# Raw expert weights issued from the sync queue, and four small moves, in a two-layer mixture-of-experts kernel

## The chip, the cores and the metric

The kernel runs on one core of a Trainium2 chip. The metric is the device time of one launch in microseconds. The engines of the core are TensorE (PE in the profile), VectorE (DVE), ScalarE (ACT), GpSimd (POOL) and the sync engine (SP); each runs its own list of instructions in order and waits on semaphores. SP and ACT can each put DMA transfers on a hardware queue of their own, GpSimd on a software queue.

## What is computed

An input of 16 images, 256 channels and 16x16 pixels goes through two layers. Each has a token mixer (a gated group convolution in the first, a 1x1 convolution in the second) and then a feed-forward network with eight experts, of which every token takes two. What matters here is the second feed-forward network, and the 1x1 convolution ahead of it:

```python
x = x + _L1_conv_ref(_ln_c(x), L1_conv_weight, L1_conv_bias)
t = _to_tokens(x)
t = t + _L1_ffn_ref(_ln_t(t), L1_ffn_gate_w, L1_ffn_gate_b, L1_ffn_w1, L1_ffn_b1, L1_ffn_w2, L1_ffn_b2)
# inside _L1_ffn_ref: 4096 tokens, d=256, F=1024, E=8, K=2
router = jax.nn.softmax(xf @ gate_w + gate_b, axis=-1)
k_scores, k_idx = jax.lax.top_k(router, K)
for i in range(e):
    h = jax.nn.silu(xf @ w1[i] + b1[i])
    y = h @ w2[i] + b2[i]
    out = out + y * comb[:, i:i + 1]
```

The first feed-forward network has the same routing, F=512 and a gated form, silu(x w1) * (x w3), then w2.

## The kernel before

Both networks are computed sparsely, and `f` is 0 in the first and 1 in the second. `route(f)` chooses experts and makes lists of the tokens of each expert, padded to tiles of 256 tokens; here that gives 35 tiles in each network, and a table `bounds` with the first tile of each expert. The loops over experts are unrolled, the loops over an expert's tiles are hardware loops whose ends are read from `bounds` at run time.

A tile `n` goes through these hands. GpSimd gathers its 256 rows from HBM (`fetch`, two indirect DMAs, for the two halves r of a tile; the first three tiles in `first_fetch`, the rest in a loop). SP turns them with two DMA transposes (`turn_rows`) into one of four buffers of `x_cols` (`RING` is 4): it turns tile n+4 once TensorE has finished the first products of tile n (`z_ready`). TensorE does the first products (L809) and the second ones (L824 in the first network, L836 in the second). ScalarE applies Silu (L1141, L1146) and scales results (L1122, L1161), VectorE splits the hidden values into a high and a low half in fp16 (L1692, L1695) and takes the result out of PSUM (L1707). GpSimd adds the result rows to `rows_y` in HBM (`put`, two indirect DMAs with addition, L562). In the second network there is only one result buffer `y_rows`: VectorE's L1707 of a tile waits (`y_free`) until both puts of the tile before have landed.

TensorE multiplies fp16 pairs, so every expert's weights are needed as high and low halves. The second network's weights are 2 MB per expert; three raw buffers `raw_v` hold them as fp32, and expert e uses buffer e % 3. `load_raw(eng, e)` issues four DMAs of 512 KB (lines 319 and 322). Expert 0 is split between the layers, the halves of expert e+1 are made one small part per tile while expert e runs (`loop_highs` on ScalarE, `loop_lows` on VectorE, counted by `part_lo`), and what is left over is done by VectorE in `rest_of` ahead of the next expert's tiles.

Where the raw weights are issued, before: ScalarE issues expert 0 behind the tiles of expert 0 of the first network (last lines of `experts`), experts 1, 2 and 3 in `route(1)` between `deviation(3, 0)` and `result_columns(5)`, and experts 4 to 7 in `next_raw` at the head of experts 1 to 4.

Other places in question: GpSimd loads the second gate's bias `gate_b` (first network) and the result biases `b2_all` (1 MB, second network) between `first_fetch(1)` and `first_fetch(2)`, and VectorE waits for them at the head of `experts`. TensorE's first products of the first network wait for a count (`hid_ready`) that VectorE sets behind that wait. SP loads the row `bias_rows` ahead of `load_tokens(0)`, which brings the tokens back between the layers; GpSimd adds that row to the tokens (L619).

## Time and profile before

| | us |
|---|---|
| median of 3 timed runs | 1178.34 (1178.17 to 1178.98) |
| profiled execution, its own time | 1181.54 |
| its span | 1179.8 |
| TensorE busy | 883.0 (75%) |
| VectorE busy | 752.3 (64%) |
| ScalarE busy | 583.7 (49%) |
| GpSimd busy | 504.1 (43%) |
| first network's tiles begin | 313.5 |
| second network's tiles begin | 758.5 |

Times of rows are in us from the start of the span. In a row of the timeline stand the start, the length, the engine, the line, the operation, what it writes and reads, how many instructions were merged into the row, and in brackets how long the engine had been idle before it and who ended that. In a row of the chain (the chain of work that ended last, followed back from the end) stand the start, the length and what it was. "q" behind an engine's name is its sequencer, which issues DMAs and takes its own time for that.

### The profile page before, as it was taken

Reading aid. Unit: us, or ns where it says so; the run is one execution under the profiler, and the core shown is the slowest. Engines: PE = TensorE matmul, PEld = TensorE weight load, DVE = VectorE, ACT = ScalarE, POOL = GpSimd, SP = SyncE. Lnnn points to the kernel's source line nnn. Section 1 sums busy time; section 2 is a strip of 40 time slices with the busy share of each in tenths; the row PEclk is TensorE's granted clock in tenths of the full one; section 3 lists DMA queues with packets and bytes.
Section 4 is the critical chain, followed back from the end, with each engine's and each line's share of the span. In section 5 each row is a group of like instructions: output and inputs, shape, how many; then the busy total and the mean of one; then the engine's idle time right before and its main releaser. Section 6 shows DMA issues by size and latency. Waiting matters only on the chain.

```text
span 1179.8 us, 25135 instructions
## 1 busy us (share of the span) xinstructions
PE 883.0 (75%) x7033; PEld 743.8 (63%) x7033; DVE 752.3 (64%) x1826; ACT 583.7 (49%) x1251; POOL 504.1 (43%) x412
## 2 busy tenths in 40 slices
PE   5321186865597999999956344499999999999975
PEld 4101165861386888888845231287888888888863
DVE  5999788989342444444446589467676677667540
ACT  4447285854162454444442247255455456555433
POOL 1288000000344676666663120245565555556540
PEclk8755598975598999999987775599999999999996
DMA  8249265982246555555654646336546464344438
GB/s 259 72 143 320 71 234 177 285 268 46 64 80 120 103 98 99 99 102 94 103 86 146 213 143 153 86 72 139 134 76 143 92 122 77 71 72 76 76 61 286
DMA packets 196628, 152.23 MB, mean 129 GB/s; under 512 B 97056, under 2 KB 181480, under 8 KB 196456
## 3 DMA queue, kind: packets, MB, share of 16 engines
q1 hardware_dynamic: 143736, 91.70, 27.6%
q0 software_dynamic: 27472, 38.97, 19.8%
q10 hardware_dynamic: 25376, 21.04, 6.3%
q8 instruction: 20, 0.33, 0.1%
q14 instruction: 24, 0.20, 0.1%
HBM read 92.35 MB, written 39.91 MB: 112 GB/s over the span
## 4 chain that ended last, share of the span: by engine, by line
PE 38%; DMA 22%; DVE 18%; issue 10%; SPq 4%; ACT 4%; ACTq 2%; POOL 1%; DVEq 1%; POOLq 0%
PE bank L836 15%; PE bank L809 13%; DMA columns<-region 8%; DMA region<-rows_x,region 7%; SPq L416 3%; PE bank L891 2%; DVE columns L1287 2%; DVE region L1266 2%; PE bank L713 2%; DVE region L1264 1%; DMA rows_y<-region 1%; DVE wreg L1632 1%; PE bank L791 1%; DVE wreg L260 1%; DMA out_dram<-columns 1%
## 5 line engine op out<-in xcount | busy, mean ns | idle before, releaser
L809 PE MATMUL bank<-columns,wreg 128*128 x3360 | 384.9, 275 | 37.0 <-DMA columns<-region 22.7
L809 PEld LDWEIGHTS bank<-columns,wreg 128*128 128x128 f16 x3360 | 331.3, 99 | 80.1 <-issue 38.5
L562 POOL DMA_INDIRECT rows_y<-region x140 | 240.5, 1718 | 166.7 <-ACT region L1161 98.5
L509 POOL DMA_INDIRECT region<-rows_x,region x148 | 156.6, 1058 | 261.1 <-DVE region L1564 144.8
L836 PE MATMUL bank<-wreg,region 128*128 128x256 f16 x1680 | 189.3, 273 | 12.4 <-DVE region L1695 12.4
L836 PEld LDWEIGHTS bank<-wreg,region 128*128 128x128 f16 x1680 | 163.2, 98 | 34.7 <-DVE region L1695 15.7
L1146 ACT ACTIVATE region<-bank,b_t,wreg 128x256 f32<-128x256 f32 x280 | 136.5, 562 | 35.8 <-PE bank L809 35.8
L1700 DVE TENSOR_TENSOR region<-region 128x256 f16<-128x256 f32 x140 | 50.1, 421 | 106.2 <-ACT region L1153 106.2
L1695 DVE SCALAR_TENSOR_TENSOR region<-region,wreg 128x512 f16<-128x512 f32 x140 | 105.3, 752 | 5.0
L1161 ACT ACTIVATE region<-region 128x256 f32<-128x256 f32 x70 | 31.8, 500 | 154.1 <-DVE region L1707 154.1
L824 PE MATMUL bank<-wreg,region 128*128 (+1 forms) x864 | 100.2, 273 | 1.9 <-ACT region L1153 1.9
L1692 DVE TENSOR_SCALAR region<-region,wreg 128x512 f16<-128x512 f32 x140 | 70.5, 504 | 46.3 <-ACT region L1146 46.3
L1141 ACT ACTIVATE region<-bank,fac 128x256 f32<-128x256 f32 x140 | 62.3, 474 | 67.4 <-PE bank L809 67.3
L824 PEld LDWEIGHTS bank<-wreg,region 128*128 128x128 f16 x864 | 84.4, 98 | 12.0 <-ACT region L1153 2.2
L1122 ACT ACTIVATE region<-bank,region 128x256 f32 x72 | 30.2, 471 | 100.3 <-DMA rows_y<-region 81.0
L1689 DVE SCALAR_TENSOR_TENSOR region<-bank,fac,region 128x256 f32<-128x256 f32 x140 | 58.9, 478 | 10.0 <-ACT region L1141 10.0
L557 POOL COPY region<-routed 128x4 uint32 x70 | 60.8, 869 | 7.3 <-DMA region<-rows_x,region 7.3
L769 PE MATMUL bank<-columns 128*128 128x160 f16 x128 | 38.6, 314 | 32.4 <-DVE columns L1538 28.3
L947 ACT ACTIVATE wreg<-wreg 128x1024 f32<-128x1024 f32 x56 | 58.5, 1053 | 2.6 <-DMA wreg<-in_L_ffn_w_dram 2.2
L1707 DVE SCALAR_TENSOR_TENSOR region<-bank,wreg,region 128x512 f32<-128x512 f32 x35 | 26.3, 751 | 49.4 <-PE bank L836 42.0
L891 PE MATMUL bank<-conv_wt,columns 128*128 128x272 f32 x128 | 37.2, 442 | 24.9 <-DVE wreg L1394 24.9
L1586 DVE SCALAR_TENSOR_TENSOR wreg<-wreg (+1 forms) x68 | 47.7, 747 | 6.3 <-ACT wreg L1091 4.2
(284 smaller groups left out, 1148.9 us busy)
## 6 DMA issues: line engine op xcount, KB each, us to landing
wreg<-in_L_ffn_w_dram SPq DMA_DIRECT2D x80, 512.0 KB, 5.8
wreg<-in_L_ffn_w_dram ACTq DMA_DIRECT2D x32, 512.0 KB, 7.4
rows_x<-region SPq DMA_DIRECT2D x16, 512.0 KB, 6.9
rows_y<-tok SPq DMA_DIRECT2D x16, 512.0 KB, 6.8
tok<-rows_y SPq DMA_DIRECT2D x16, 512.0 KB, 6.0
wreg<-in_x_dram SPq DMA_DIRECT2D x4, 1024.0 KB, 9.8
out_dram<-columns ACTq DMA_DIRECT2D x16, 256.0 KB, 2.4
region<-rows_x,region POOLq DMA_INDIRECT x148, 2.9
```

The lines of the kernel that those rows point to most:

```text
L509: nc.gpsimd.indirect_dma_start(x_bits[:, b, r, 0:C + 2], None, rows_x[f], bass.IndirectOffsetOnAxis(ap=row_list, axis=0)).then_inc(xr_load ...
L557: nc.gpsimd.tensor_copy(now[:, b], moves[:, bass.ds(2 * t, 2), :]).then_inc(lists_copied[f], 1)
L562: nc.gpsimd.indirect_dma_start(rows_y[f], bass.IndirectOffsetOnAxis(ap=now[:, b, g_, 1:2], axis=0), (y_pair[:, b], y_rows)[f][:, g_, :], N ...
L809: last = pe.matmul(to, block, x_cols[:, bass.ds(b, 1), :, xs_, k, :].rearrange("p j r n -> p (j r) n"), start=(k == 0 and ws_ + xs_ == 0), ...
L824: last = pe.matmul(yb[:, r * C:(r + 1) * C], lhs[:, r * P:(r + 1) * P], w2_of(c, ws_), start=(c == 0 and r == 0 and hs + ws_ == 0), stop=( ...
L836: last = pe.matmul(yb[:, r * C:(r + 1) * C], lhs[:, c, r * P:(r + 1) * P], v_s[:, e % 2, c // 2, 1, ws_, (c % 2) * C:(c % 2 + 1) * C], sta ...
L891: last = pe.matmul(zb[2 * j + h][:, 0:C + 2 * E], xt[:, j, k, h * P:(h + 1) * P], conv1_wt[:, k], start=(k == 0), stop=(k == KC - 1))
L1141: act.activation(gate_act[:, h, (c % 2) * TILE:(c % 2 + 1) * TILE], zb[c][:, 0:TILE], ACT.Silu, scale=fac[f][:, 0, e:e + 1]).then_inc(silu ...
L1146: last = act.activation(gate_act[:, h, c * TILE:(c + 1) * TILE], zb[h][:, c * TILE:(c + 1) * TILE], ACT.Silu, bias=b1_t[:, e, 2 * h + c:2 ...
L1689: dve.scalar_tensor_tensor(half(hid[:, h], c), zb[c][:, TILE:2 * TILE], fac[f][:, 1, e:e + 1], half(gate_act[:, h], c), ALU.mult, ALU.mult ...
L1692: dve.tensor_scalar(to_hi, gate_act[:, h], fac[f][:, 1, e:e + 1], None, ALU.mult).then_inc(hi_ready[f], 1)
L1695: dve.scalar_tensor_tensor(to_lo, gate_act[:, h], fac[f][:, 1, e:e + 1], to_hi, ALU.mult, ALU.subtract).then_inc(lo_ready[f], 1)
```

## The change

It has five parts. The raw weights are issued by SP: expert 0 ahead of the turning loop of the first network, experts 1 and 2 behind `load_tokens(0)`, expert 3 ahead of the turning loop of the second network, experts 4 to 7 behind the turns of experts 0 to 3, once the parts of the last tile are made. VectorE's wait for `gate_b` stands behind the first network's tiles, and its wait for `b2_all` at the head of `experts` is gone (the wait in front of L1707 counts the same semaphore). `first_fetch(2)` stands ahead of the loads of `gate_b` and `b2_all`. ScalarE does one Silu of one column ahead of the tiles. The row `bias_rows` is loaded behind the fourth of the eight token loads.

```diff
             def load_tokens(f):
                 for i in range(HB):
+                    if f == 0 and i == 4:
+                        sp.dma_start(bias_rows[:], ...).then_inc(bias_loaded, 16)
...
+            def turn_behind(f, first, end):
+                with sp.Fori(first, end) as n:
+                    sp.wait_ge(z_ready[f], 4 * n + 4)
+                    turn_rows(f, n + RING)
             def turn_tiles(f):
...
-                with sp.Fori(0, total + 2 - RING) as n:
-                    sp.wait_ge(z_ready[f], 4 * n + 4)
-                    turn_rows(f, n + RING)
+                if f == 0:
+                    sp.wait_ge(w_lo, 6 * E)
+                    load_raw(sp, 0)
+                    turn_behind(0, 0, total + 2 - RING)
+                else:
+                    sp.wait_ge(v_lo, 4)
+                    load_raw(sp, 3)
+                    edges = [sp.value_load(bounds[0:1, e:e + 1], min_val=0, max_val=TILES) for e in range(5)]
+                    for e in range(4):
+                        turn_behind(1, edges[e], edges[e + 1])
+                        with sp.Fori(edges[e + 1], edges[e + 1] + 1) as n:
+                            sp.wait_ge(part_lo, n + 1)
+                        load_raw(sp, e + 4)
+                    turn_behind(1, edges[4], total + 2 - RING)
...
-            sp.dma_start(bias_rows[:], ...).then_inc(bias_loaded, 16)
             load_tokens(0)
+            for e in (1, 2):
+                load_raw(sp, e)
...
                 first_fetch(1)
+                first_fetch(2)
                 if f == 0:
                     (loads of gate_b)
                 else:
                     pool.dma_start(b2_all, b2.partition_broadcast(P)).then_inc(y_free, 16)
-                first_fetch(2)
...
                     deviation(3, 0)
-                    for e in (1, 2, 3):
-                        load_raw(act, e)
                     result_columns(5)
...
             def experts(f, edges):        # ScalarE
                 act.wait_ge(fac_ready[f], 1)
+                act.activation(spare_column, fac[f][:, 0, 0:1], ACT.Silu)
...
-                    if f == 1 and 0 < e and e + 3 < E:
-                        next_raw(e + 3, edges[e])
...
-                    if f == 0 and e == 0:
-                        load_raw(act, 0)
...
             def experts(f, edges):        # VectorE
-                for loaded in (y_put, [y_free])[f]:
-                    dve.wait_ge(loaded, 16)
...
             experts(0, edges)
+            for b in range(2):
+                dve.wait_ge(y_put[b], 16)
             first_lows()
```

ScalarE in `route(1)`, before, between the layers. L995 is `result_columns`, L921 a square root of `deviation`, L1005 and L1009 are `result_rows`, L319 and L322 `load_raw`:

```order
L995 ACTIVATE columns<-bank 128x512 x6
L921 ACTIVATE rstd<-var 128x16
L319 DMA wreg<-in_L_ffn_w_dram 128x2x512 x2
L322 DMA wreg<-in_L_ffn_w_dram 128x4x256 x2
L319 DMA wreg<-in_L_ffn_w_dram 128x2x512 x2
L322 DMA wreg<-in_L_ffn_w_dram 128x4x256 x2
L319 DMA wreg<-in_L_ffn_w_dram 128x2x512 x2
L322 DMA wreg<-in_L_ffn_w_dram 128x4x256 x2
L995 ACTIVATE columns<-bank 128x512 x2
```

And with the change (the same lines are L1016, L942, L1026 and L1030):

```order
L1016 ACTIVATE columns<-bank 128x512 x6
L942 ACTIVATE rstd<-var 128x16
L1016 ACTIVATE columns<-bank 128x512 x2
L1026 ACTIVATE wreg<-tok,mean,rstd 128x256 x4
L1030 ACTIVATE region<-wreg 128x2x256 x2
```

Twelve DMA instructions no longer stand between the square root and the columns.

SP in the second network, before, from the turns of tile 3 into the turning loop:

```order
L416 DMA_TRANSPOSE columns<-region 128x4x128 [waits xr_loaded0_1,xc_ready0_1]
L416 DMA_TRANSPOSE columns<-region 128x4x128 [waits xr_loaded1_1,xc_ready1_1]
L426 UNCONDITIONAL_BRANCH
L426 ISA
L265 ISA [waits z_ready1]
```

With the change, from the turns of the last tile of expert 0's loop to the head of expert 1's (L419 is the turn, L445 the wait for the parts, L320 and L323 are `load_raw`):

```order
L419 DMA_TRANSPOSE columns<-region 128x4x128
L419 ISA [waits xr_loaded1_1,xc_ready1_1]
L419 DMA_TRANSPOSE columns<-region 128x4x128
L423 REGISTER_ALU
L423 COMPARE_AND_BRANCH
L445 UNCONDITIONAL_BRANCH
L445 ISA
L445 ISA [waits part_lo]
L445 COMPARE_AND_BRANCH
L320 DMA wreg<-in_L_ffn_w_dram 128x2x512 x2
L323 DMA wreg<-in_L_ffn_w_dram 128x4x256 x2
L423 UNCONDITIONAL_BRANCH
```

The four loads stand behind the turns of the tile that is four ahead of the expert's last one, and ahead of every later turn.

ScalarE at the head of the second network's tiles, before and then with the change:

```order
L1135 UNCONDITIONAL_BRANCH
L1135 ISA
L1146 ACT_TABLE_LOAD
L1146 ACTIVATE region<-bank,b_t,wreg 128x256 x2
```

```order
L1142 ACT_TABLE_LOAD
L1142 ACTIVATE wreg<-wreg 128x1
L1147 UNCONDITIONAL_BRANCH
L1147 ISA
L1158 ACTIVATE region<-bank,b_t,wreg 128x256 x2
```

The load of the table stood inside the loop over expert 0's tiles and now stands ahead of it; the first network's shows the same.

## Rows read from the trace of the kernel before

**Rows 1.** Timeline of TensorE, first network, tile 0 and the one stall.

```profile
313.54 8.26 PE L809 MATMUL bank<-columns,wreg 128*128 x48 [13.74 <-DVEq L1668]
...
364.47 6.73 PE L809 MATMUL bank<-columns,wreg 128*128 x48 [8.61 <-DMA columns<-region]
...
373.65 5.40 PE L809 MATMUL bank<-columns,wreg 128*128 x48
```

**Rows 2.** Chain of work, first network: gate bias, and a turn at the stall.

```profile
309.75 3.54 DMA gate_b<-in_L_ffn_gate_b_dram
352.33 11.75 DMA columns<-region
```

**Rows 3.** Line 416 (the turns) in the window 307.7 to 309: issue, then landing.

```profile
L416 SPq DMA_TRANSPOSE columns<-region x2: 1250/1280/1309, 306.6 to 308.0; - x2
DMA to landing us min/median/max: 3.3/3.3/3.3
```

**Rows 4.** Timeline of ScalarE: first raw DMA of expert 0.

```profile
349.38 0.69 ACTq L319 DMA_DIRECT2D wreg<-in_L_ffn_w_dram  x1
```

**Rows 5.** Timeline of GpSimd: the first put of the first network.

```profile
334.75 1.67 POOL L562 DMA_INDIRECT rows_y<-region  x1 [11.70 <-ACT region L1122]
```

**Rows 6.** Timelines of ScalarE, then VectorE, between the layers.

```profile
668.02 1.09 ACT L995 ACTIVATE columns<-bank 128x512 f32<-128x512 f32 x2 [11.69 <-issue]
...
675.24 0.25 DVE L1215 RECIPROCAL st_lg<-wreg 128x16 f32<-128x16 f32 x1 [9.93 <-ACT wreg L921]
```

**Rows 7.** Chain of work: last put of network one, bias row; turn at network two.

```profile
612.59 3.96 DMA rows_y<-region
617.74 0.37 SPq L436
...
753.28 4.93 DMA columns<-region
```

**Rows 8.** Timelines, second network, expert 0: TensorE, then ScalarE's table load.

```profile
777.11 5.45 PE L836 MATMUL bank<-wreg,region 128*128 128x256 f16 x48 [0.46 <-DVE region L1695]
788.25 5.41 PE L836 MATMUL bank<-wreg,region 128*128 128x256 f16 x48 [0.45 <-DVE region L1695]
...
773.42 1.28 ACT L1146 ACT_TABLE_LOAD   x1
```

**Rows 9.** Timeline of TensorE at the change to expert 5, which has no load.

```profile
1000.64 5.41 PE L836 MATMUL bank<-wreg,region 128*128 128x256 f16 x48 [1.76 <-DVE region L1695]
```

**Rows 10.** Timeline of VectorE: first split behind the change to experts 1 to 4.

```profile
810.95 0.48 DVE L1692 TENSOR_SCALAR region<-region,wreg 128x512 f16<-128x512 f32 x1 [0.72 <-ACT region L1146]
844.24 0.49 DVE L1692 TENSOR_SCALAR region<-region,wreg 128x512 f16<-128x512 f32 x1 [1.50 <-ACT region L1146]
899.68 0.48 DVE L1692 TENSOR_SCALAR region<-region,wreg 128x512 f16<-128x512 f32 x1 [1.18 <-ACT region L1146]
943.71 0.49 DVE L1692 TENSOR_SCALAR region<-region,wreg 128x512 f16<-128x512 f32 x1 [1.28 <-ACT region L1146]
```

**Rows 11.** Timeline of TensorE: second stall behind a change of expert.

```profile
857.28 5.41 PE L836 MATMUL bank<-wreg,region 128*128 128x256 f16 x48 [1.06 <-DVE region L1695]
911.98 5.41 PE L836 MATMUL bank<-wreg,region 128*128 128x256 f16 x48 [0.31 <-DVE region L1695]
956.79 5.41 PE L836 MATMUL bank<-wreg,region 128*128 128x256 f16 x48 [1.09 <-DVE region L1695]
```

**Rows 12.** Chain of work: a put beside a raw load that began at 895.8.

```profile
899.26 8.57 DMA rows_y<-region
```

**Rows 13.** Timelines of TensorE and GpSimd, an undisturbed tile of the second network.

```profile
867.77 5.40 PE L836 MATMUL bank<-wreg,region 128*128 128x256 f16 x48
878.16 1.86 POOL L562 DMA_INDIRECT rows_y<-region  x1 [0.30 <-issue]
883.12 0.98 POOL L509 DMA_INDIRECT region<-rows_x,region  x1 [0.30 <-issue]
```

**Rows 14.** The page's DMA issues: all gathers, median us to landing.

```profile
region<-rows_x,region POOLq DMA_INDIRECT x148, 2.9
```

More of the change, by code:

```diff
@@ L118, in bass_metaformer @@
         marks = region[:, 7861:7863]
+        spare_column = wreg[:, 32464:32465]
         raw_at = (24576, 16384, 20480)
@@ L389, in load_tokens @@
                 for i in range(HB):
+                    if f == 0 and i == 4:
+                        sp.dma_start(bias_rows[:], bias.rearrange("c a -> (c a)").partition_broadcast(P)).then_inc(bias_loaded, 16)
                     if i >= 4:
@@ L435, in _ @@
                     sp.wait_ge(waited, each * m + more)
-            sp.dma_start(bias_rows[:], bias.rearrange("c a -> (c a)").partition_broadcast(P)).then_inc(bias_loaded, 16)
             load_tokens(0)
+            for e in (1, 2):
+                load_raw(sp, e)
             for waited, each, more in ((xc_ready[0][0], 16, 32), (xc_ready[1][0], 16, 32)):
@@ L1107, in loop_highs @@
                 part_highs(e, (n - first) % 4).then_inc(part_hi, 1)
-            def next_raw(e, first):
-                with act.Fori(first, first + 1) as n:
-                    act.wait_ge(part_lo, n + 1)
-                load_raw(act, e)
             def result_of_last(n):
```

## The prediction

> **What bounds the kernel now.** I read the page's 40 slices first, then the chain of work, then each engine's timeline where the chain leaves TensorE. Four things hold TensorE or VectorE up, and raw loads or their neighbours stand beside all four.
>
> In the first network TensorE begins at 313.54, behind a wait of VectorE [rows 1], and the chain shows what that was: the gate bias, issued at 309.75, landing 3.54 later [rows 2]. Tile 5 then begins after 8.61 us idle, and its first products last 6.73 where those of the next tile last 5.40, at a lower granted clock [rows 1]. The chain has a turn issued at 352.33 that took 11.75 to land [rows 2], where a turn of the first tile took 3.3 [rows 3]; ScalarE had issued 2 MB of raw weights from 349.38 on [rows 4].
>
> Between the layers ScalarE's next arithmetic behind its twelve raw DMAs comes at 668.02, after 11.69 idle that is put down to issue (so from 656.3 on), and VectorE waited 9.93 for the square root behind it, until 675.24 [rows 6]. From there to the second network the chain is mostly VectorE's routing, which the change leaves alone.
>
> In the second network TensorE is the bound where nothing disturbs it: 5.24 us for each half of a tile, 10.48 a tile (each row shows 5.40, as ends are modelled) [rows 13]. It loses a little in expert 0, at every change of expert, and once more a tile later.
>
> **The change part by part.** All terms are us against the profiled execution (1181.54 for a span of 1179.8); the median of the runs is 1178.34, and I take the same difference off the median.
>
> Gate bias: VectorE no longer waits. What is late next is the turn of tile 0: the second transpose is issued at 308.0 and lands 3.3 later [rows 3], 311.3, so TensorE starts near 311.6: gain 1.9. GpSimd now waits for the bias itself ahead of its first list, some 1 to 2 us behind that tile's gather, but its first put comes only at 334.75 after 11.70 idle [rows 5]; that idle time hides it.
>
> Raw expert 0: SP issues it behind the turns of tile 3. The gather of tile 3 is GpSimd's last ahead of that idle time, which begins at 323.05 (334.75 less 11.70) [rows 5]; it lands 2.9 after its issue [rows 14], so the load starts near 327 less the 1.9 won. It lasts some 12 us (a put beside such a load landed 12.1 behind its start, below), so it is nearly through when the gather behind the first pair of puts starts, and a result is double buffered here. The stall goes: 8.61 and the slow 1.33 (6.73 less 5.40) [rows 1], 9.9 in all. If gather 4 is caught by its end I lose up to 3.
>
> Bias row: one issue of 0.37 less ahead of the token loads [rows 7], 0.4. GpSimd needs it only after VectorE's first statistics, so its later landing is hidden.
>
> Raw experts 1 to 3 leave ScalarE. Its work from 668.02 to VectorE's start at 675.24 is 7.2 us; started at 656.4 it ends at 663.6, before VectorE asks at 665.3 (675.24 less 9.93) [rows 6]. What is late next is VectorE itself, then a usual wait of some 0.3: gain 9.6. Experts 1 and 2 now follow the token loads on SP, where nothing is waited for until VectorE's first fp16 rows are stored, and those come behind the square root.
>
> Result biases: the turn that starts the second network took 4.93 beside 1 MB of them [rows 7]; 3.3 is the nearest undisturbed one [rows 3]: gain 1.6. They are next needed by the first L1707, more than a tile's 10.48 after TensorE's start.
>
> Silu table: ScalarE loads it in every pass of expert 0's loop, 1.28 each. In the second network tiles there are 11.14 apart (777.11 to 788.25) [rows 8], against 10.48: 0.66 for three tiles, 2.0. In the first network TensorE has no gap there: nothing.
>
> ScalarE's loads at the changes to experts 1 to 4: VectorE's first split waited 0.72, 1.50, 1.18 and 1.28 for ScalarE [rows 10], together 4.7 (4.68). VectorE's `rest_of` is late next and no load helps that: the change to expert 5 has no load and still costs 1.76 [rows 9].
>
> Sum of gains: 1.9 + 9.9 + 0.4 + 9.6 + 1.6 + 2.0 + 4.7 = 30.1.
>
> What it adds: five raw loads (experts 3 to 7) run in the second network where four did, and at another moment. Count from E, the end of a tile's second products (873.0 in the undisturbed tile). Its second put is issued at E+5.15, the gather four tiles on at E+10.1 [rows 13], landing 2.9 later [rows 14], near E+13; only then does SP get past the turns of that tile and issue the raw load. E of the next tile is 10.5 (10.9 at a change of expert) later, so the raw load starts 3.7 after it and the next pair of puts is issued 0.6 before and 1.4 behind its start. VectorE's L1707 needs those puts at 10.6. Undisturbed a put lands in 3.96 [rows 7], at 9.1, in time. Beside a raw load begun at 895.8 it took 8.57 from 899.26 [rows 12], so it landed 12.1 behind the load's start. By the length it lands at 5.15 + 8.57 = 13.7, 3.1 late; by the raw load's end at 3.7 + 12.1 = 15.8, 5.2 late. Against this, the raw load now follows the turns instead of sharing with them, so it may be through sooner. About 0.8 of lateness is slack (a put 2 us late cost TensorE 1.06 and 1.09 [rows 11]). So a stall lies between 0 and 4.4 for each load; I take 2.3, what the row's own length gives: 5 x 2.3 = 11.5. The three old stalls of 1.06, 0.31 and 1.09 [rows 11] go, 2.5. Net loss 9.0. The turns behind a raw load are one to two tiles late at most, and the ring holds them three tiles ahead.
>
> 30.1 less 9.0 is 21.1, and 1178.3 less 21.1 is 1157.2.
>
> A rule speaks to the sharing. The row shows a turn on SP's queue held for 11.75 behind a raw load on ScalarE's [rows 2, 4]. The Trainium skill, "DMA: Bandwidth & Descriptors", section "Queues, rings and completion order", says that each DMA engine goes round the queues it has work for, packet by packet, while one queue is consumed in order. By that a short turn on a queue of its own should have landed long before the end of the load, which the row does not bear out. For a put it would mean that it lands ahead of the raw load's end once the turns share the load's queue; that is the first rival.
>
> **The rivals.** *Puts keep their pace.* With load and turns on one queue, the put's queue has one competitor instead of two; it lands at 10.6 to 12 and a stall costs what the old ones did, 2.5/3 = 0.8. Then 5 x 0.8 - 2.5 = 1.6 is lost and 28.5 gained: 1149.8. For it: only three of four old loads stalled a second time. Against: 8.57 at 899.26 [rows 12]. The skill's rule of round robin points here.
>
> *Every put waits for the load's end.* If that is 13 behind its start, the put lands at 16.7, 6.1 late, a stall is 5.3: 26.5 - 2.5 = 24.0 lost, 6.1 gained: 1172.2.
>
> *Slower than before.* The same mechanism with a longer load: what is issued beside it lands with its end, and SP's queue serves it more slowly than ScalarE's. Break-even is a stall of (30.1 + 2.5)/5 = 6.5, a put landing 14.2 behind the load's start. At 16 the stall is 8.3: 41.5 - 2.5 - 30.1 = 8.9 lost, 1187.2. Against: beside the old load nothing in the rows took longer than 11.75 [rows 2] or landed later than 12.1 to 14.7 behind its start (352.33 + 11.75 less 349.38).
>
> *The change does not free ScalarE between the layers.* If the square root waits for something else there, 9.6 is missing: 1166.8. Against: the 11.69 idle is put down to issue, with no releaser, and the DMAs fill it [rows 6].
>
> **How the numbers follow.** Forecast 1157.2 (1152 to 1162 with its own bounds) 0.45; puts keep their pace, 1149.8, 0.25; puts wait for the end, 1172.2, 0.17; ScalarE not freed 0.05; slower 0.04; the rest for things in between. The range takes in the first rival with the 2.5 of stalls gone altogether (30.1 + 2.5 is 1145.7, half way to it is 1147) and stops at 1170 just short of the second. Faster by over 0.2% (2.4 us, what a measurement here can tell from no change) 0.94, within it 0.02, slower 0.04.
>
> **What would show it.** First network: TensorE's start near 311.6, no idle time near 355, ScalarE's table load once. Between the layers VectorE's reciprocal waits about 0.3 instead of 9.93. Second network: no table load in the loop and tiles of expert 0 10.5 apart, but a stall of L836 in the second or third tile behind every raw load, with VectorE's L1707 waiting for a put; the sum of these over five loads is 11.5 in the forecast, 4 in the first rival, 26 in the second. The forecast is wrong if gaps of over 3 us remain in the first network, if VectorE waits for a raw buffer at a change of expert, or if TensorE waits for turns in the second.

## The result and the profile after

| | before | after | forecast |
|---|---|---|---|
| median of 4 runs, us | 1178.66 | 1152.18 (1151.83 to 1153.16) | 1157.2 (1147 to 1170) |
| profiled execution, its own time | 1181.54 | 1153.16 | |
| its span | 1179.8 | 1151.4 | |

The ratio is 0.977, 95% interval 0.974 to 0.980: 26.5 us were gained where 21.1 were forecast. The two profiled spans lie 28.4 apart, since the profiled execution of before was 2.9 above its median and that of after 1.0 above its own.

I cut both traces at the same seven places. "Gather" is GpSimd's first gather of a network, "tiles" run from TensorE's first product to the end of its last second product, "tokens" is TensorE's first work on the tokens between the layers.

| stretch, us | before | after | gained | forecast |
|---|---|---|---|---|
| start to gather 1 | 303.57 | 300.51 | 3.1 | none |
| gather 1 to first product | 9.97 | 8.33 | 1.6 | 1.9 |
| tiles of network 1 | 294.51 | 284.39 | 10.1 | 9.9 |
| end of them to tokens | 16.17 | 14.00 | 2.2 | 0.4 |
| tokens to gather 2 | 124.69 | 116.03 | 8.7 | 9.6 |
| gather 2 to first product | 9.60 | 7.97 | 1.6 | 1.6 |
| tiles of network 2 | 384.19 | 383.05 | 1.1 | -2.3 |
| behind them | 37.1 | 37.1 | 0 | 0 |

The first row is not the change's. It varies from 298.0 to 304.2 over all kernels below, with and without any part of the change. Most of the 3.1 arises between 200 and 270 us, and the granted clock differs there. Which of the two causes the other is not shown (one kernel below has 303.1 at a clock of 0.63). The windows' table has length, TensorE busy (instructions), granted clock, DMA share and GB/s; before, then after:

```profile
240.00:300.00 60.00, 35.85 (x165) 0.59 0.45 135
```

```profile
240.00:300.00 60.00, 31.62 (x169) 0.63 0.45 137
```

The other rows come from one execution of each kernel, and the repeat of after (below) shows how far they hold: there the tiles of network 1 took 287.4 and those of network 2 380.9, so these two gains were 7.1 and 3.3 instead of 10.1 and 1.1; the other rows behind the first agree within 0.2.

In after L830 holds the first products (L809 before), L845 and L857 the second ones, L419 the turns, L320 and L323 the raw loads, L583 the puts, L530 the gathers, L1700 and L1703 VectorE's splits, L1715 its result, L942 the square root.

TensorE's and VectorE's timelines of after, against [rows 1], [rows 6] and [rows 8]:

```profile
350.74 5.40 PE L830 MATMUL bank<-columns,wreg 128*128 x48
...
607.23 1.97 PE L903 MATMUL bank<-ident,tok 128*128 128x128 f32 x8 [14.01 <-DMA tok<-rows_y]
...
649.64 0.25 DVE L1225 RECIPROCAL st_lg<-wreg 128x16 f32<-128x16 f32 x1 [0.28 <-ACT wreg L942]
...
731.23 6.76 PE L830 MATMUL bank<-columns,wreg 128*128 x48 [11.72 <-DMA columns<-region]
```

Tile 5 begins at 350.74 without idle time and at full pace: the stall of 8.61 and its slow pass are gone. The reciprocal waits 0.28 where it waited 9.93. In the second network TensorE still waits, for VectorE's splits, in ten places and 10.9 in all:

```profile
761.13 7.08 PE L857 MATMUL bank<-wreg,region 128*128 128x256 f16 x48 [2.19 <-DVE region L1703]
...
785.69 5.41 PE L857 MATMUL bank<-wreg,region 128*128 128x256 f16 x48 [1.75 <-DVE region L1703]
...
808.29 5.42 PE L857 MATMUL bank<-wreg,region 128*128 128x256 f16 x48 [1.47 <-DVE region L1703]
...
841.36 5.41 PE L857 MATMUL bank<-wreg,region 128*128 128x256 f16 x48 [1.03 <-DVE region L1703]
...
873.40 5.41 PE L857 MATMUL bank<-wreg,region 128*128 128x256 f16 x48 [0.43 <-DVE region L1703]
```

The rows at 785.69 and 873.40 are changes of expert; those at 761.13, 808.29 and 841.36 come behind a raw load (of experts 3, 4, 5), as do two more of 0.79 and 1.02 behind experts 6 and 7. The products that begin at 761.13 also ran slow (7.08 against 5.40); the granted clock was 0.76 from 761 to 768 and 1.00 from 768 to 775.

Why: SP's load of expert 4 and GpSimd's puts, and the wait of VectorE's result behind them.

```profile
793.37 1.24 SPq L320 DMA_DIRECT2D wreg<-in_L_ffn_w_dram  x2
...
794.01 1.78 POOL L583 DMA_INDIRECT rows_y<-region  x1 [4.61 <-ACT region L1173]
...
796.09 1.86 POOL L583 DMA_INDIRECT rows_y<-region  x1 [0.30 <-issue]
...
804.17 0.75 DVE L1715 SCALAR_TENSOR_TENSOR region<-bank,wreg,region 128x512 f32<-128x512 f32 x1 [3.76 <-DMA rows_y<-region]
```

The load itself: its last two DMAs, with the time from issue to landing. The last one was issued at 795.3 and landed 9.1 later, at 804.4:

```profile
L323 SPq DMA_DIRECT2D wreg<-in_L_ffn_w_dram x2: 498/554/610, 794.7 to 795.3; - x2
DMA to landing us min/median/max: 7.4/8.2/9.1
```

And the puts in the chain of work of after, one for each of the five loads:

```profile
748.24 8.75 DMA rows_y<-region
...
796.09 8.05 DMA rows_y<-region
...
829.60 7.61 DMA rows_y<-region
...
883.81 7.37 DMA rows_y<-region
...
927.10 7.60 DMA rows_y<-region
```

### The profile page after: what moved, and what is told of

It is laid out like the page before. It is cut to its first block, busy times and chain, and to the rows that moved or that the text cites. A ratio compares the mean times of both kernels' runs of the same rounds, so it can differ in the third digit from the quotient of the medians.

```text
span 1151.4 us, 25150 instructions
## 1 busy us (share of the span) xinstructions
PE 877.9 (76%) x7033; PEld 739.3 (64%) x7033; DVE 754.3 (66%) x1826; ACT 576.0 (50%) x1247; POOL 503.8 (44%) x412
## 3 DMA queue, kind: packets, MB, share of 16 engines
q1 hardware_dynamic: 156536, 108.48, 32.9%
## 4 chain that ended last, share of the span: by engine, by line
PE 33%; DMA 24%; DVE 22%; issue 10%; SPq 4%; ACT 2%; DVEq 2%; POOL 1%; ACTq 1%; POOLq 0%
PE bank L857 14%; PE bank L830 11%; DMA columns<-region 8%; DMA region<-rows_x,region 8%; DMA rows_y<-region 4%; SPq L419 3%; PE bank L912 2%; DVE columns L1297 2%; DVE region L1276 2%; DVE region L1274 2%; PE bank L734 1%; DVE wreg L1642 1%; DVE columns L1246 1%; DVE wreg L261 1%; DMA tok<-rows_y 1%
## 5 line engine op out<-in xcount | busy, mean ns | idle before, releaser
L830 PE MATMUL bank<-columns,wreg 128*128 x3360 | 382.4, 274 | 25.3 <-DMA columns<-region 13.0
L830 PEld LDWEIGHTS bank<-columns,wreg 128*128 128x128 f16 x3360 | 330.1, 98 | 66.8 <-issue 26.6
L583 POOL DMA_INDIRECT rows_y<-region x140 | 242.5, 1732 | 158.5 <-ACT region L1173 98.4
L530 POOL DMA_INDIRECT region<-rows_x,region x148 | 155.6, 1052 | 252.0 <-DVE region L1574 141.3
L857 PE MATMUL bank<-wreg,region 128*128 128x256 f16 x1680 | 190.9, 274 | 10.9 <-DVE region L1703 10.9
L857 PEld LDWEIGHTS bank<-wreg,region 128*128 128x128 f16 x1680 | 164.3, 98 | 33.5 <-DVE region L1703 13.9
L1703 DVE SCALAR_TENSOR_TENSOR region<-region,wreg 128x512 f16<-128x512 f32 x140 | 105.2, 751 | 5.0
L845 PE MATMUL bank<-wreg,region 128*128 (+1 forms) x864 | 100.2, 273 | 1.9 <-ACT region L1165 1.9
L1700 DVE TENSOR_SCALAR region<-region,wreg 128x512 f16<-128x512 f32 x140 | 70.7, 505 | 40.3 <-ACT region L1158 40.1
L845 PEld LDWEIGHTS bank<-wreg,region 128*128 128x128 f16 x864 | 84.4, 98 | 12.0 <-ACT region L1165 2.2
L1715 DVE SCALAR_TENSOR_TENSOR region<-bank,wreg,region 128x512 f32<-128x512 f32 x35 | 26.3, 751 | 58.2 <-PE bank L857 40.5
L790 PEld LDWEIGHTS bank<-columns 128*128 128x128 f16 x128 | 13.3, 104 | 58.3 <-DVE columns L1548 49.0
```

The lines of the kernel that those rows point to most:

```text
L530: nc.gpsimd.indirect_dma_start(x_bits[:, b, r, 0:C + 2], None, rows_x[f], bass.IndirectOffsetOnAxis(ap=row_list, axis=0)).then_inc(xr_load ...
L583: nc.gpsimd.indirect_dma_start(rows_y[f], bass.IndirectOffsetOnAxis(ap=now[:, b, g_, 1:2], axis=0), (y_pair[:, b], y_rows)[f][:, g_, :], N ...
L830: last = pe.matmul(to, block, x_cols[:, bass.ds(b, 1), :, xs_, k, :].rearrange("p j r n -> p (j r) n"), start=(k == 0 and ws_ + xs_ == 0), ...
L845: last = pe.matmul(yb[:, r * C:(r + 1) * C], lhs[:, r * P:(r + 1) * P], w2_of(c, ws_), start=(c == 0 and r == 0 and hs + ws_ == 0), stop=( ...
L857: last = pe.matmul(yb[:, r * C:(r + 1) * C], lhs[:, c, r * P:(r + 1) * P], v_s[:, e % 2, c // 2, 1, ws_, (c % 2) * C:(c % 2 + 1) * C], sta ...
L1700: dve.tensor_scalar(to_hi, gate_act[:, h], fac[f][:, 1, e:e + 1], None, ALU.mult).then_inc(hi_ready[f], 1)
```

## The experiments

The runs of one kernel spread over 1 to 9 us, so the medians and ratios tell the large parts only. Each kernel was therefore also cut as above; the short stretches that an edit doesn't touch agree much better (gather 1 to first product 8.2 to 8.5, end of tiles to tokens 13.9 to 14.2). The tiles of network 1 do not: 283.3 to 287.4, with one to four waits of 0.5 to 1.9 for a turn that differ from trace to trace. I also cut network 2 in two, at the second products with which expert 1 begins: in after the part ahead of this change took 54.5 and the part behind it 328.6, in its repeat 52.5 and 328.4. Ratios are to the kernel before on the same chip, with their 95% intervals. All edits are to the kernel after.

**Experts 1 to 3 back on ScalarE.**

```diff
-            for e in (1, 2):
-                load_raw(sp, e)
...
-                    sp.wait_ge(v_lo, 4)
-                    load_raw(sp, 3)
...
                     deviation(3, 0)
+                    for e in (1, 2, 3):
+                        load_raw(act, e)
                     result_columns(5)
```

> The kernel after with one part undone: raw experts 1, 2 and 3 are issued by ScalarE again between deviation(3, 0) and result_columns(5). The kernel after took 1152.2. Forecast's theory (ScalarE's issues hold back the square root): VectorE's reciprocal waits some 10 us again, the gap between the layers grows by 9.6; expert 3 no longer runs beside the first tiles of the second network, where it cost 2.19 idle and 1.7 at a lower clock in the trace of after, so 9.6 - 3.9 = 5.7 in all, 1157.9. Rival (the square root waits for something else): the reciprocal waits under 1 us and only the 3.9 shows, 1148.3.

Measured: 1164.28, ratio 0.988 (0.986 to 0.990). Tokens to gather 2 took 127.90 instead of 116.03, the tiles of network 2 383.06 instead of 383.05. ScalarE, then VectorE:

```profile
646.73 3.46 ACTq L320 DMA_DIRECT2D wreg<-in_L_ffn_w_dram  x2
650.23 2.82 ACTq L323 DMA_DIRECT2D wreg<-in_L_ffn_w_dram  x2
653.15 1.08 ACT L1012 ACTIVATE columns<-bank 128x512 f32<-128x512 f32 x2 [12.99 <-issue]
...
660.37 0.25 DVE L1223 RECIPROCAL st_lg<-wreg 128x16 f32<-128x16 f32 x1 [11.23 <-ACT wreg L938]
```

The mechanism is the forecast's: the issues hold ScalarE, and through the square root VectorE. The cost is not a constant. The first pair of these issues took 1.34 here, the last two 3.46 and 2.82. The 3.9 that I took off for expert 3 came where I expected it (up to the change to expert 1 the network took 50.5, in after 54.5) and was lost again: the same stall with a slow pass (1.95 and 7.08) stood behind the load of expert 4 instead.

**Expert 0 back on ScalarE.**

```diff
                 if f == 0:
-                    sp.wait_ge(w_lo, 6 * E)
-                    load_raw(sp, 0)
                     turn_behind(0, 0, total + 2 - RING)
...
+                    if f == 0 and e == 0:
+                        load_raw(act, 0)
```

> The kernel after with one part undone: raw expert 0 is issued by ScalarE again, behind the tiles of expert 0 of the first network. Forecast's theory (the load, begun while the turns of tile 5 are on their way, held them up): TensorE is idle 8.6 at tile 5 with a slow first half of 1.3 behind it, 9.9 in all, 1162.1. Rival (what held the turn up was the gather or the state of the queue at that place, not the load): no idle time over 2 us at that tile and 1152.2 to 1154.

Measured: 1163.48, ratio 0.986 (0.984 to 0.989). The tiles of network 1 took 295.43; in all kernels without this edit they took 283.3 to 287.4. ScalarE's issue, the turn in the chain of work and TensorE:

```profile
347.32 0.70 ACTq L320 DMA_DIRECT2D wreg<-in_L_ffn_w_dram  x1
```

```profile
350.40 10.84 DMA columns<-region
```

```profile
361.63 8.28 PE L828 MATMUL bank<-columns,wreg 128*128 x48 [7.83 <-DMA columns<-region]
```

As forecast: 7.83 idle and 2.88 in a slow pass (8.28 less 5.40), 10.7. The turn, with a load on another queue 3 us ahead of it, took 10.84.

**The waits for the biases back.**

```diff
                 first_fetch(1)
-                first_fetch(2)
...
                     pool.dma_start(b2_all, ...).then_inc(y_free, 16)
+                first_fetch(2)
...
             def experts(f, edges):        # VectorE
+                for loaded in (y_put, [y_free])[f]:
+                    dve.wait_ge(loaded, 16)
```

> The kernel after with one part undone: VectorE waits for gate_b and b2_all at the head of experts and GpSimd fetches the third tile behind those loads. Forecast's theory: TensorE starts 1.9 later in the first network (behind the bias, issued and landing in 3.5) and 1.6 later in the second (its first turn takes 4.9 instead of 3.3), 3.5 in all, 1155.7. Rival (the earlier start is given back within the network, since the ring of four tiles is filled by GpSimd and SP at the old pace): the starts move by that, the ends of the networks do not, 1152.2.

Measured: 1162.65, ratio 0.987 (0.985 to 0.989). Gather 1 to first product is 9.96, the value of before. The tiles of network 1 took 284.42, which lies in the range of the other kernels, so no part of the 1.6 is seen to be given back, and none above the spread of 4 can be excluded. Gather 2 to first product is 8.32 (7.97 in after, 9.60 in before), but the tiles of network 2 took 385.92, 2.9 more. The bias's DMA in the chain, then VectorE and TensorE:

```profile
732.03 6.73 DMA region<-in_L_ffn_b_dram
```

```profile
738.78 0.17 DVE L1668 TENSOR_TENSOR region<-region 128x4 f32<-128x4 f32 x1 [12.56 <-DMA region<-in_L_ffn_b_dram]
...
742.41 0.48 DVE L1702 TENSOR_SCALAR region<-region,wreg 128x512 f16<-128x512 f32 x1
...
743.74 7.08 PE L857 MATMUL bank<-wreg,region 128*128 128x256 f16 x48 [2.03 <-DVE region L1705]
```

VectorE waited for the result biases until 738.78, did 3.6 of other work, and its first split came 2.03 too late for TensorE, whose next pass was slow. Of the 1.6 between gather 2 and the first product this kernel gives back only 0.35, although its turn met the biases as in before. There the biases were issued 1.1 behind the second turn (753.28 and 754.39), and TensorE began 5.2 behind that turn [rows 7]. Here, with the turn issued at 731.0 and the biases at 732.03, it began 3.9 behind:

```profile
L419 SPq DMA_TRANSPOSE columns<-region x2: 1247/1262/1278, 729.6 to 731.0; - x2
```

```profile
734.85 6.86 PE L830 MATMUL bank<-columns,wreg 128*128 x48 [12.07 <-DMA columns<-region]
```

In before VectorE's wait was covered: TensorE's first pass there was itself late and slow (7.66 from 758.51), and VectorE was just in time. So the wait was dearer than it looked, once the turn ahead of it was short: 2.03 idle and 1.7 of a slow pass at this place. The profiled run lies 6.6 above the profiled one of after: 1.6, 0.4 and 2.9 in the places named, and 1.4 between tokens and gather 2, which the edit does not touch. The median lies 10.5 above, and the other runs have no trace, so the rest is open.

**The order alone.** The same without VectorE's waits:

```diff
                 first_fetch(1)
-                first_fetch(2)
...
                     pool.dma_start(b2_all, ...).then_inc(y_free, 16)
+                first_fetch(2)
```

> The kernel after with the third tile fetched behind the loads of gate_b and b2_all, as before, but without VectorE's waits. With both undone the first products came 1.6 later in the first network, and in the second VectorE waited for b2_all until 738.78, TensorE then 2.03 for its split, with a slow pass behind it: 1.6 + 1.7 + 2.9 in all. If the waits make that, here it is gone: gather to first product 8.3 and the second network's tiles 380 to 383, 1152 to 1153. If the place of the loads makes it (1 MB in front of the third tile's gather and beside the turns), 2.9 or more of it stays in the second network, 1156.

Measured: 1154.65, ratio 0.978 (0.975 to 0.981). Gather 1 to first product 8.29, tiles of network 2 383.04, no idle time at the first tile. Gather 2 to first product is 8.61, where ten traces with the new order have 7.97 to 8.14. One with the new order (expert 0 back on ScalarE) has 8.50, though, so the 0.5 to 0.6 that 1 MB beside the turns would cost is not clear of the spread. The late first products of network 1 and the stall of 2.03 in network 2 are the waits' doing: both are gone here.

**No Silu ahead of the tiles.**

```diff
                 act.wait_ge(fac_ready[f], 1)
-                act.activation(spare_column, fac[f][:, 0, 0:1], ACT.Silu)
```

> The kernel after with one part undone: no Silu of one column ahead of the tiles. Forecast's theory: a table load of 1.28 stands in every pass of expert 0's loop again, the second network's tiles of expert 0 are 11.1 apart instead of 10.5, 2.0 in all with nothing in the first network, 1154.2. Rival 1 (the halves' parts of a tile are ScalarE's and VectorE's slack anyway and the last tile catches up): 1152.5. Rival 2 (the first network's tiles also wait for ScalarE): over 1155.

Measured: 1155.47, ratio 0.981 (0.977 to 0.985). The tiles of network 1 took 285.09, as elsewhere: nothing there. In network 2 the table load is back in each pass, and TensorE loses 0.46, 0.63 and 0.45 behind them:

```profile
748.99 1.28 ACT L1157 ACT_TABLE_LOAD   x1
...
760.31 1.28 ACT L1157 ACT_TABLE_LOAD   x1
...
771.41 1.28 ACT L1157 ACT_TABLE_LOAD   x1
```

```profile
775.09 5.41 PE L857 MATMUL bank<-wreg,region 128*128 128x256 f16 x48 [0.45 <-DVE region L1702]
```

From the first product to the change to expert 1 it takes 52.5, against 50.4 to 50.6 in the three kernels without a raw load in that stretch: 2.0, as forecast, if the load of expert 3, which stands in that stretch too, cost nothing in this trace. Over the whole second network it does not show (382.71 against 383.05 and 380.93), since what the load of expert 3 costs there varies more.

**The bias row back ahead of the tokens.**

```diff
-                    if f == 0 and i == 4:
-                        sp.dma_start(bias_rows[:], ...).then_inc(bias_loaded, 16)
...
+            sp.dma_start(bias_rows[:], ...).then_inc(bias_loaded, 16)
             load_tokens(0)
```

> The kernel after with one part undone: SP loads bias_rows ahead of load_tokens(0) again. Forecast's theory: 0.37 of issue more, 1152.6, and TensorE's first transpose of tokens comes 0.4 later behind SP's wait for the last puts. Rival (the broadcast to 128 partitions stands in the queue ahead of the first tokens and delays their landing): TensorE's first work on the tokens comes 1.6 to 2.2 later, of which some 1 reaches the end, 1153.2 to 1154.4.

Measured: 1155.35, ratio 0.979 (0.974 to 0.983). End of tiles to tokens is 16.07; with the row behind, 13.9 to 14.2 in every other kernel here. SP, and TensorE behind it:

```profile
604.37 0.36 SPq L454 DMA_DIRECT2D routed<-in_L_conv_bias_dram  x1
604.79 10.67 SPq L393 DMA_DIRECT2D tok<-rows_y  x8
```

```profile
610.62 1.97 PE L902 MATMUL bank<-ident,tok 128*128 128x128 f32 x8 [16.08 <-DMA tok<-rows_y]
```

TensorE starts 5.83 behind the issue of the first token load; in after that is 4.28 (602.95 to 607.23). So the row's transfer costs 1.6 and its issue 0.4. The rival was right. Up to gather 2 the kernel is 2.4 longer than after and 2.6 longer than its repeat; in its median it does not stand out from the spread.

**Experts 4 to 7 back on ScalarE.**

```diff
-                    for e in range(4):
-                        turn_behind(1, edges[e], edges[e + 1])
-                        ...
-                        load_raw(sp, e + 4)
-                    turn_behind(1, edges[4], total + 2 - RING)
+                    turn_behind(1, 0, total + 2 - RING)
...
+                    if f == 1 and 0 < e and e + 3 < E:
+                        next_raw(e + 3, edges[e])
```

> The kernel after with one part undone: raw experts 4 to 7 are issued by ScalarE again, one part into experts 1 to 4, as before (expert 3 stays on SP ahead of the turning loop). Forecast's theory in its own sizes: VectorE waits for ScalarE at the four changes again, 4.7 more, and the four stalls of 2.3 go for three of 0.8, 6.7 less: 1150.2. By the sizes of the trace of after (stalls of 1.47, 1.03, 0.79 and 1.02 behind the loads of experts 4 to 7, 4.3 in all): 4.7 + 2.5 - 4.3 = 2.9 more, 1155.1. Rival (the changes cost the same whoever issues, since VectorE's rest_of is what is late): 1152.2 - 4.3 + 2.5 = 1150.4, with VectorE's first split behind each change waiting under 0.5.

Measured: 1155.01, ratio 0.978 (0.975 to 0.981); tiles of network 2 383.88, 331.0 of them behind the change to expert 1 (328.6 in after). The idle times of TensorE at the four changes were 2.24, 1.66, 1.69 and 1.45, together 7.0, where after has 1.75, 0, 0.43 and 0.23, together 2.4: 4.6, and I had 4.7. Behind these changes stood 0.65 and 0.75, where after has 4.3 behind its loads. 4.6 + 1.4 - 4.3 = 1.7 more idle time than after, and the 2.24 had a slow pass of 7.08 behind it: of what moving these four loads off ScalarE won, most went back into waits for puts. The chain of this kernel has puts of 8.81 and 8.73 beside ScalarE's loads. Beside SP's they took 7.4 to 8.8 in after, 8.0 to 8.7 in a kernel below and 6.6 to 8.9 in all the chains, so no effect of the load's queue on a put's length is shown.

**Tiny loads for experts 3 to 7.**

```diff
             raw = raw_v[e % 3]
+            if e in (3, 4, 5, 6, 7):
+                for k in range(4):
+                    eng.dma_start(raw[:, k, 0, 0:4], v1[e, 0:P, 4 * k:4 * k + 4]).then_inc(raw_loaded[e % 3], 16)
+                return
```

> The kernel after with the raw loads of experts 3 to 7 replaced by four transfers of a few columns each, at the same places and with the same counts; the raw weights of those experts are not loaded, so the second network computes experts 3 to 7 with what is left in the buffers. It bounds what the loads cost beside the second network's tiles. Forecast's theory (puts beside a load land late): the idle time behind each load goes, 5 x 2.3 = 11.5, 1140.7. By the trace of after: 2.19 + 1.7 of a slow pass for expert 3 and 1.47 + 1.03 + 0.79 + 1.02 for the others, 8.2, 1144.0. Rival (those stalls are not the loads' but belong to that tile behind a change of expert, the rest_of having put VectorE behind): 1148 to 1152.

This kernel leaves out the raw weights of experts 3 to 7 and computes them with what is left in the buffers; it only bounds what the loads cost. Measured: 1145.69, ratio 0.971 (0.969 to 0.974). Tiles of network 2 373.63. TensorE waits 4.3 in all, at the changes of expert and not a tile behind them; the puts in the stretch where those of after took 7.8 to 8.1 give:

```profile
DMA to landing us min/median/max: 3.9/4.1/4.3
```

So the five loads cost 383.05 - 373.63 = 9.4 in the trace of after, and 7.3 in that of its repeat. The part behind the change to expert 1 is 323.2 here: the loads of experts 4 to 7 cost 5.4 and 5.2 of that, and the rest, 4.0 and 2.1, lies in the part with expert 3's load.

**Two halves a tile apart.**

```diff
-                        turn_behind(1, edges[e], edges[e + 1])
+                        turn_behind(1, edges[e] + 1 if e else 0, edges[e + 1])
...
-                        load_raw(sp, e + 4)
+                        load_raw(sp, e + 4, (0,))
+                        turn_behind(1, edges[e + 1], edges[e + 1] + 1)
+                        load_raw(sp, e + 4, (1,))
```

> The kernel after with experts 4 to 7 loaded in two halves: the first two DMAs at the same place, the other two behind the next tile's turns. If a put is late by the length of what it shares with, a half of the load makes it half as late: the put stands 2.2 to 3.1 later than undisturbed now and would be 1.1 to 1.6 later, which is about VectorE's slack, so the four stalls of together 4.3 go to under 1: 1148.5. Rival (a put is late by the same amount beside any load, because each tile's puts now meet one of the two halves): twice as many stalls of half the size, 1152. Other side (the second half comes later and the parts of the next expert or the turns behind it become late): over 1154.

Measured: 1148.16, ratio 0.974 (0.971 to 0.978). Tiles of network 2 374.38, nearly what tiny loads give. Not all of the 8.7 is the edit's: behind the change to expert 1 the network took 323.9, which is 4.7 less than in after, and the other 4.1 is the load of expert 3, still whole, which cost nothing in this trace. The stall behind the load of expert 4 and the put ahead of it:

```profile
815.90 5.41 PE L859 MATMUL bank<-wreg,region 128*128 128x256 f16 x48 [0.40 <-DVE region L1705]
```

```profile
804.77 5.76 DMA rows_y<-region
```

A put beside a half took 5.76 and 6.96 where it was late at all, and VectorE's slack took in nearly all of that.

**One tile later, whole.**

```diff
-                        turn_behind(1, edges[e], edges[e + 1])
+                        turn_behind(1, edges[e] + 1 if e else 0, edges[e + 1])
...
-                        load_raw(sp, e + 4)
+                        turn_behind(1, edges[e + 1], edges[e + 1] + 1)
+                        load_raw(sp, e + 4)
```

> The kernel after with experts 4 to 7 issued whole, behind the next tile's turns instead of this one's (where the second halves stood). It tells the size of a load from its moment: by size, the same 2 MB stand beside a later tile's puts and the stalls of 0.8 to 1.5 stay, only one tile later, the second network at 380 to 384 and 1152; by moment (the tile right behind a change of expert is the tight one, since VectorE has just done the rest of the halves), they go as with the halves, 374 to 376 and 1147.

Measured: 1156.14, ratio 0.979 (0.976 to 0.982). Tiles of network 2 383.41. The stalls moved one tile on and grew, to 3.05, 2.10, 1.56 and 1.37 (8.1, against 4.3):

```profile
817.92 6.84 PE L858 MATMUL bank<-wreg,region 128*128 128x256 f16 x48 [3.05 <-DVE region L1704]
```

```profile
804.13 8.42 DMA rows_y<-region
...
840.23 8.69 DMA rows_y<-region
...
895.51 8.14 DMA rows_y<-region
...
939.62 7.96 DMA rows_y<-region
```

So the stalls go with the whole load and not with the tile behind a change of expert. The moment matters as well: behind the change to expert 1 the network took 333.1 where after has 328.6.

**The kernel after once more, and a version with both.** The version has the halves, and expert 3 issued between the layers:

```diff
-                    sp.wait_ge(v_lo, 4)
-                    load_raw(sp, 3)
...
             for e in (1, 2):
                 load_raw(sp, e)
+            sp.wait_ge(v_lo, 4)
+            load_raw(sp, 3)
```

> The kernel after once more, unchanged, beside the other three of this call. The traces so far differ by up to 5 us in the time of the first gather (299.1 to 304.2), which no part of the change touches, and by 0 to 4 us in what the load of expert 3 costs in the first tiles of the second network. Expected: 1152 to 1155; the stretches first gather to first product (8.3), first network's tiles (284), tiles to tokens (14.0) and tokens to the next gather (116) within 0.5 of the first trace; the second network's tiles 380 to 383, with stalls of 1.0 to 1.5 after the changes of expert again.

> The kernel after with experts 4 to 7 loaded in two halves a tile apart and expert 3 issued behind experts 1 and 2 between the layers instead of ahead of the second network's turning loop. The halves alone gave 1148.2 and a second network of 374.4 (383.1 in the trace of after, 373.6 with tiny loads). If expert 3 costs something in the second network, its place between the layers gives that back: 1 to 4 less than the halves, 1145 to 1147. Rival (10 MB now stand in SP's queue ahead of the layer's rows, which are stored from 655 on and would land later, up to the first gather of the second network): tokens to gather over 118 instead of 116, 1150 or more.

Measured, on one chip: the kernel after 1153.83 (0.979, 0.976 to 0.981), the version 1147.77 (0.972, 0.970 to 0.975), 0.5% faster than after. Its tiles of network 2 took 375.24, tokens to gather 2 117.54 (115.83 in the repeat of after). So the halves give the gain, and moving expert 3 gives none that shows: with it ahead of the turning loop the stretch from the first product to the change to expert 1 took 50.4 to 54.5 in eight traces (those without edits in that stretch), without it 50.4 to 50.6. It costs nothing in some executions and 4 in the profiled one of after. In these eight traces its cost follows the moment of the load. Issued 3.4 to 5.1 behind the end of the network's first products it left no idle time (three traces), issued 5.4 to 6.3 behind them 0.3 to 0.7 (three), at 6.7 it cost 1.75 and at 8.0, in after, 2.19 with a slow pass. No run moved this load alone, so this is a correlation.

## Why the forecast was right, point by point

- **Gate bias**, 1.9 forecast, 1.6 measured (9.97 to 8.33, and 9.96 with the wait back). Right; no part of it is seen to be given back.
- **Expert 0**, 9.9 forecast, 10.1 in the trace (7.1 in the repeat) and 8 to 12 by undoing it (295.43 against 283.3 to 287.4). Right, with its reason: the stall itself, idle and slow pass, is 9.9 in before, 10.7 with the load back, and gone without it. What varies is the small waits for turns elsewhere.
- **Bias row**, 0.4 forecast, 2.2 measured. The failed step: I counted only its issue of 0.37 [rows 7] and wrote that its landing was hidden, since nobody needs the row early. But its transfer stands in the queue ahead of the tokens, for which TensorE waits.
- **Experts 1 to 3**, 9.6 forecast. VectorE's wait fell from 9.93 to 0.28, which is 9.65; 8.7 of it reached gather 2. The missing 1.0 stands ahead of it: from tokens to the square root of `deviation(3, 0)` it takes 31.9 in before and 32.9 in after (656.11 less 624.22, 640.15 less 607.23). It is 32.8 to 33.9 in all kernels of the experiments, with the bias row back ahead of the tokens too (32.8) and with experts 1 to 3 back on ScalarE (33.7), so neither move alone explains it; it stays open. Bias row and experts 1 to 3 together: 10.0 forecast, 10.8 measured.
- **Result biases**, 1.6 forecast, 1.6 in the trace, but only 0.35 and 0.64 came back when the old place was restored. So 1.0 or more of it is not shown to be the change's, and that the sum met the 1.6 here is luck: the forecast put all of a turn's 4.93 against 3.3 down to the biases, and the same biases left the turn short in the experiment. The step was also too narrow: the turn, which I costed, hid a wait of VectorE, which costs 2.9 more once the turn is short.
- **Silu table**, 2.0 forecast, 2.0 measured in the second network if expert 3's load cost nothing there (1.5 of it is idle time that the trace shows), nothing in the first.
- **ScalarE at the changes**, 4.7 forecast, 4.6 measured.
- **Collisions.** This is the term that was mis-sized. Forecast 11.5 for five loads, measured 9.4 and 7.3. Here is where 2.1 of the difference lies. The mechanism was right: an L1715 waits 3.76 for a put of 8.05. I had the put at 8.57 [rows 12] and 3.1 late with 0.8 slack, 2.3 a load; expert 4's was 2.7 late (804.17 less the end of the products at 801.4) and cost 1.47, so the slack was 1.3; the load was issued 2.3 behind the end of the products (793.37 less 791.1) and not 3.7; four loads cost 4.3 idle, and expert 3's 2.19 and 1.7.
- Before had more to give in the second network than my terms: it is 10.6 above tiny loads, and I had 2.0 + 4.7 + 2.5 = 9.2. Of the 1.4, 0.9 is its first pass (7.66 against 6.74), at a granted clock of 0.70 against 0.80.

Together: 3.4 in the second network and 1.8 for the bias row, less 0.9 for experts 1 to 3 and 0.1 elsewhere, are the 4.2 by which the untouched start aside the trace gained more (25.3) than forecast (21.1). The rival "puts keep their pace" was nearer in time, 1149.8 against a median of 1152.2. Counted from the end of the products, as the forecast did, expert 4's second put landed at 13.0 (804.1 less 791.1): the forecast had 13.7, the rival 10.6 to 12. So the put did not keep its pace. But the idle time behind the loads of experts 4 to 7 was 1.1 on average, nearer to the rival's 0.8 than to my 2.3, and all five loads together cost 1.5 to 1.9 each. "Every put waits for the load's end" and the slower case needed later landings: expert 4's second put landed 10.8 behind the start of its load, not 12.1 to 16. But the loads were shorter than that rival assumed, too: 10.1 to 11.2 instead of 13. Set against the real end of its load, the second put landed 0.3 and 0.2 ahead of it for experts 3 and 4, and 2.0, 1.9 and 2.5 ahead for experts 5 to 7; the first put of each pair landed 2.2 to 8.1 ahead. So puts do not wait for the end in general, but the two dearest landings cannot be told from such a wait. "ScalarE not freed" is refuted by the 0.28.

On the sharing, what the rows show: a put that takes 4.0 alone took 6.6 to 8.9 beside a load (second puts in the chains of all kernels, both queues), and 5.6 to 7.1 beside half a load. The Trainium skill, "DMA: Bandwidth & Descriptors", section "Queues, rings and completion order", has each DMA engine go round its queues packet by packet. I read that as speaking for a put that keeps its pace. Two queues that take turns in equal shares would make a put about twice as long, which agrees with these lengths; that the shares are equal is my inference, and no run here shows it. It does not explain the turn, which took 3.3 alone and 10.84 to 11.75 beside a load; this stays open.

## What to carry to other kernels

A DMA issue on a compute engine is that engine's time, more of it behind several MB of loads, and costs what waits behind it; a transfer that nobody waits for still costs what stands behind it in its queue. Where a small transfer with a deadline runs in every tile, cut the large ones beside it so that what they add stays within its slack (here 4.7 for four loads). When a delay is taken away, look for a second wait that ended just ahead of it: the one for 1 MB of biases cost nothing beside a slow turn, and 2.9 without it.

## What the runs showed of the hardware

- The issues of DMAs get slower as loads pile up in a queue. ScalarE's twelve issues took 11.8 in before and 13.1 with experts 1 to 3 back on it: the first pair 1.34, the fifth 3.46. SP shows the same in after behind the token loads: pairs of 1.26, 3.65, 2.57 and 2.88.

```profile
612.07 1.26 SPq L320 DMA_DIRECT2D wreg<-in_L_ffn_w_dram  x2
613.37 3.65 SPq L323 DMA_DIRECT2D wreg<-in_L_ffn_w_dram  x2
```

- A row that is broadcast to 128 partitions, ahead of a 512 KB load in the same queue, put off that load's landing by 1.6 (from issue to TensorE's start 5.83 against 4.28).
- A stall costs more than its idle time: behind seven waits of 1.95 to 3.05 TensorE's next pass took 6.8 to 7.1 instead of 5.40 (granted clock 0.76 in after), though behind two of 2.10 and 2.33 it took 5.4; behind the 7.83 in the first network it took 8.28, at a granted clock of 0.64.
